# A fused deformable-convolution, attention and expert block: joined edits in the group norm, the hats, the tap products and the gated experts

## The chip, the core and the metric

The kernel runs on one core of one Trainium2 chip. Its engines are TensorE (PE; its weight loads are listed apart as PEld), VectorE (DVE), ScalarE (ACT), GpSimd (POOL) and SyncE (SP), which here only issues DMAs. Each engine works through its own list of instructions, and semaphores tie the lists together. The metric is device microseconds of one execution, the median of several runs. The kernel before takes 83.26 us.

## What is computed

The input x is 8 images of 16x16 pixels with 32 channels, all float32. Cut to what matters:

```python
x = x + conv(_gn(x), ...)          # group norm: each channel of each image over its 256 pixels
t = to_tokens(x)
t = t + attention(_ln_t(t))        # scores x x^T, softmax, weighted sum, per image
t = t + experts(_ln_t(t), ...)     # 8 experts of 32x32, the best two of each token, gated

def conv(x, ...):                  # a deformable 3x3 convolution, 8 groups of 4 channels
    x_proj = x @ w_in + b_in
    x1 = gelu(layer_norm(depthwise_3x3(x) + dw_b) * ln_g + ln_b)
    offset = x1 @ w_off + b_off                    # 8 groups x 9 taps x 2 coordinates
    mask = softmax((x1 @ w_msk + b_msk), over the 9 taps)
    # each tap reads x_proj at its place plus its offset, bilinearly; weighted by mask, summed
    return out @ w_out + b_out
```

## The kernel before

All data stay on the chip. The program is written out by hand: five lists, one for each engine, in the order in which they run, with a semaphore for each hand-over. Nothing schedules them afterwards, so an instruction that waits holds up all that stand behind it on its engine. The stages that the change touches are these.

**Group norm** (5 to 11 us of the trace). TensorE transposes the rows. VectorE takes BN_STATS of even and odd segments into `x_stats`. TensorE's `over_segments` (L552) averages the segment means by a product with `chan_mean` (x_mean). VectorE forms `x_dev`, its square `x_devsq` (L1095) and `x_segvar` (L1096, the segment variances plus these squares); TensorE averages that (x_var), ScalarE makes `gn_rstd` from it, and VectorE scales all columns to `xnT` in one instruction (L1102). Then TensorE runs the depthwise convolution as 12 products (L576). Between its real products stand warm products, whose results nobody reads (`keep_warm`, L538, counts in `WARM`). A float32 product is two records in the trace.

**Hats** (20 to 28 us). Bilinear weights of an offset o are the hats max(o,0), max(-o,0) and 1-|o|. The 16 image columns come in four chunks. VectorE makes the mask logits and the upper hat of each chunk; ScalarE makes the exponentials, |o| (`magnitudes`) and, for chunks 2 and 3 (`ACT_LOWER`), the lower hat (L923); POOL makes the middle hats and the lower hats of chunks 0 and 1. VectorE's first weight product (L309, `first_my`) waits for all of them; POOL and ScalarE then feed VectorE's second one.

**Taps** (28 to 51 us). For each of five tap rows `ty`, VectorE forms weights (`weights(i)`, L313), TensorE adds them up and turns them (`add_weights(ty)`, L643), VectorE multiplies them with the images (`products(ty)`, L1144, in pieces given by `PIECES[ty]`) and TensorE adds the products up (`add_row(ty)`, L654). Row 3 (`PAIRED`) is added in pairs on POOL (L510). `products(ty)` waits for `coef_done` of its row; each piece releases TensorE. Afterwards TensorE goes on to the tokens (L694, L718).

**Gated experts** (72 to 79 us). TensorE computes all experts of group n (L828). VectorE multiplies by the gates (`gated_experts`, L1346) for six n and ScalarE for n = 3 and 7 (L1026). VectorE sums four n over the experts (`sum_experts`, L1367) and POOL the other four in two lots (L529, L530). VectorE stores its gated values as [expert, channel]; ScalarE stores them as [channel, expert], where the eight addends lie side by side. The last result is L1382; its DMA follows.

## Time and profile before

| | us |
|---|---|
| median of 3 runs | 83.26 (83.23 to 83.63) |
| the profiled execution, its own time | 83.83 |
| its span, first to last instruction | 82.1 |
| TensorE busy | 70.6 (86%) |
| VectorE busy | 54.7 (67%) |
| POOL busy | 48.4 (59%) |
| ScalarE busy | 42.8 (52%) |

The span is what the rows below count in; 1.73 us of the profiled execution's time lie around it. TensorE's busy share holds all warm products, so it isn't the share of the work. The granted TensorE clock is full until 76 us and half from there on (0.964 on average).

### The profile page before, as it was taken

How to read it: one execution, taken by the hardware profiler on the slowest of the kernel's cores; microseconds unless marked ns; L12 is line 12 of the kernel's file. 1: busy time of each engine (PE TensorE's matmuls, PEld its weight loads, DVE VectorE, ACT ScalarE, POOL GpSimd, SP SyncE). 2: the span in 40 equal slices, each digit the busy share in tenths (PEclk: the TensorE clock that was granted, in tenths of full speed). 3: DMA queues.
4: the chain of work that ended last, by engine and by line, in shares of the span. 5: the costliest groups of instructions: out<-in, count | busy, mean ns of one | idle time of the engine just before them, and what ended most of it. 6: DMA issues, size and time to landing. Idle time of an engine off the chain costs nothing.

```text
span 82.1 us, 1760 instructions
## 1 busy us (share of the span) xinstructions
PE 70.6 (86%) x655; PEld 58.5 (71%) x655; DVE 54.7 (67%) x103; ACT 42.8 (52%) x141; POOL 48.4 (59%) x78
## 2 busy tenths in 40 slices
PE   1999999999599999899799999997797989999600
PEld 1989879867399988698799989775444767666200
DVE  1141530363996899999997996646235758999950
ACT  0353200499669256969994000365993430299910
POOL 5107089998599699999999997000003500248920
PEclk9999999999999999999999999999999999999555
DMA  0412182004870000000000000000000000000014
GB/s 0 131 43 57 26 168 28 10 8 140 241 198 0 8 4 0 0 0 4 0 0 8 4 0 0 0 0 8 0 0 0 0 0 8 0 0 0 0 33 95
DMA packets 5607, 2.51 MB, mean 31 GB/s; under 512 B 4623, under 2 KB 5135, under 8 KB 5599
## 3 DMA queue, kind: packets, MB, share of 16 engines
q1 hardware_dynamic: 4895, 2.14, 10.8%
q10 hardware_dynamic: 704, 0.26, 1.2%
q8 instruction: 5, 0.08, 0.4%
q14 instruction: 3, 0.02, 0.1%
HBM read 0.95 MB, written 0.26 MB: 15 GB/s over the span
## 4 chain that ended last, share of the span: by engine, by line
PE 26%; DVE 25%; ACT 5%; issue 3%; POOL 2%; POOLq 1%; DVEq 0%
PE ps L654 10%; DVE prod L313 6%; DVE image_all L1144 6%; DVE image_all L1346 4%; PE ps L643 4%; PE ps L775 3%; ACT image_all L1002 3%; POOL image_all L529 2%; PE ps L785 2%; PE ps L793 2%; PE ps L756 1%; DVE prod L1367 1%; PE ps L694 1%; PE ps L718 1%; PE ps L702 1%
## 5 line engine op out<-in xcount | busy, mean ns | idle before, releaser
L538 PE MATMUL ps<-wide_ident 128*128 128x128 f32 x104 | 15.8, 309 | 1.8 <-POOL wide_ident L396 1.8
L538 PEld LDWEIGHTS ps<-wide_ident 128*128 128x128 f32 x104 | 14.3, 218 | 3.2 <-POOL wide_ident L396 1.8
L1144 DVE TENSOR_TENSOR image_all<-ps,images 128x896 f32<-128x896 f32 (+4 forms) x8 | 13.2, 1690 | 0.4 <-PE ps L643 0.4
L654 PE MATMUL ps<-wide_ident,image_all 128*128 128x128 f32 (+2 forms) x92 | 11.2, 275 | 0.9 <-DVE image_all L1144 0.9
L654 PEld LDWEIGHTS ps<-wide_ident,image_all 128*128 128x128 f32 (+2 forms) x92 | 10.0, 139 | 1.6 <-DVE image_all L1144 1.6
L643 PE MATMUL ps<-wide_ident,prod 128*128 128x128 f32 x81 | 9.9, 275 | 0.1
L520 POOL TENSOR_TENSOR prod<-prod,tok 128x256 f32<-128x256 f32 x2 | 1.9, 962 | 12.9 <-DVE prod L1296 12.9
L643 PEld LDWEIGHTS ps<-wide_ident,prod 128*128 128x128 f32 x81 | 8.8, 141 | 0.8 <-DVE prod L313 0.6
L309 POOL TENSOR_TENSOR my<-prob,hat 128x384 f32<-128x384 f32 x8 | 7.9, 1012 | 0.7 <-DVE ps L309 0.7
L313 POOL TENSOR_TENSOR prod<-my,hat 128x1152 f32<-128x1152 f32 x3 | 8.0, 2652 | 0.2
L313 DVE TENSOR_TENSOR prod<-ps,hat 128x1152 f32<-128x1152 f32 x6 | 7.9, 1350 | 0.1
L1026 ACT ACTIVATE image_all<-ps,gate_s 128x32 f32<-128x32 f32 x32 | 5.9, 358 | 1.5 <-DVE gate_s L1338 1.5
L828 PE MATMUL ps<-expert,prod 32*128 32x256 f32 x32 | 4.9, 397 | 0.1
L529 POOL TENSOR_TENSOR image_all<-image_all 128x512 f32<-128x512 f32 (+1 forms) x4 | 4.0, 997 | 1.4 <-DVE image_all L1346 1.1
L975 ACT ACTIVATE sampT<-ps 128x128 f32<-128x128 f32 x2 | 0.8, 398 | 7.8 <-PE ps L718 7.8
L943 ACT ACTIVATE ps<-my 128x384 f32<-128x384 f32 x5 | 2.5, 495 | 4.0 <-POOL my L309 3.2
L828 PEld LDWEIGHTS ps<-expert,prod 32*128 32x128 f32 x32 | 3.4, 184 | 0.8 <-DVE image_all L1346 0.4
L1346 DVE TENSOR_TENSOR image_all<-ps,gate_s 128x512 f32<-128x512 f32 x6 | 3.8, 682 | 0.0
L576 PE MATMUL ps<-conv_w,xnT 128*128 128x160 f32 (+1 forms) x24 | 3.8, 316 | 0.0
L576 PEld LDWEIGHTS ps<-conv_w,xnT 128*128 128x128 f32 x24 | 3.6, 190 | 0.2 <-issue 0.2
L1107 DVE TENSOR_REDUCE c_sum<-c_sq 128x8 f32<-128x256 f32 x2 | 0.7, 414 | 4.4 <-ACT c_sq L901 4.4
L970 ACT ACTIVATE x_ctok<-x_tok,x_mean_tok 128x32 f32<-128x32 f32 x16 | 3.5, 308 | 0.0
(199 smaller groups left out, 143.9 us busy)
## 6 DMA issues: line engine op xcount, KB each, us to landing
images<-images SPq DMA_DIRECT2D x2, 300.0 KB, 4.2
images<-images SPq DMA_DIRECT2D x2, 280.0 KB, 3.6
x_tok<-in_x SPq DMA_DIRECT2D x4, 64.0 KB, 3.6
x_rows<-in_x SPq DMA_DIRECT2D x1, 128.0 KB, 2.8
x_rows<-in_x ACTq DMA_DIRECT2D x1, 128.0 KB, 3.2
expert<-in_expert_w SPq DMA_DIRECT2D x4, 32.0 KB
out_dram<-prod SPq DMA_DIRECT2D x2, 64.0 KB, 2.2
out_dram<-prod ACTq DMA_DIRECT2D x2, 64.0 KB, 2.5
```

The source lines that it names most:

```text
L309: return engine.tensor_tensor(dst, prob[:, ky:NP:K, :], hat[:, NP + ky:2 * NP:K, dy, :], ALU.mult)
L313: return engine.tensor_tensor(prod[:, ky, dy].rearrange("p (k d) j -> p k d j", d=D), bcast(rows, 2, D), hat[:, ky:NP:K, :, :], ALU.mult)
L529: then(g.tensor_tensor(x[:, :, 0:n], x[:, :, 0:n], x[:, :, n:2 * n], ALU.add))
L538: pe.matmul(pbank(bank, P), ident, ident, start=True, stop=True)
L576: ins = pe.matmul(pbank(2, (hi - lo) * C, x0 * C), xnT[:, b, dy:dy + H, :], conv_w[:, dy, lo:hi, :], start=False, stop=(b == 3 and dy == K ...
L643: ins = pe.matmul(coef_rows(ty, tx, tx + 1), prod[:, ky, dy, kx * D + dx, :], ident, start=first[tx // 4], stop=((ky, dy) == PAIRS_OF_ROW[ ...
L654: ins = pe.matmul(ps[0:last, SAMPLED, c * NJ:(c + 1) * NJ], taps[:, ty % SLOTS, tx, c, 0:last], ident, start=(ty == 0 and tx == 0 and c == ...
L828: ins = pe.matmul(pbank(EXPERT[n], NE * C, h * NE * C), ln2T[q * C:(q + 1) * C, ga, h, :], expert4[q * C:(q + 1) * C, :, :], start=True, s ...
L970: ins = act.activation(x_ctok[:, t, :], x_tok[:, ga, n, h, :], ACT.Identity, bias=x_mean_tok[:, t:t + 1])
L1026: ins = act.activation(gated_by_channel(ga, q, q + 1)[:, h, :, e], pbank(EXPERT[n], C, (h * NE + e) * C), ACT.Copy, scale=gate_s[:, ga * G ...
L1144: v.tensor_tensor(taps[:, ty % SLOTS, t0:t1, :, y0 * NI:y1 * NI], bcast(coef_rows(ty, t0, t1).rearrange("p (t j) -> p t j", j=P)[:, :, y0 ...
L1346: v.tensor_tensor(gated[:, ga, q, :, :, :], pbank(EXPERT[n]).rearrange("p (h e c) -> p h e c", h=HALVES, e=NE), bcast(by_image[:, q, :, :] ...
```

## The change

1. **Group norm.** A second matrix `chan_mean_32` (`chan_mean` / 32) is made early on. TensorE averages the segments' own sums of squares with it right behind x_mean, into bank 5, and adds the average of `x_devsq` to the same sum later; `x_segvar` is gone. The warm products behind x_mean fall from 4 to 3 and the one ahead of the convolution goes. `xnT` is written in two halves, and the convolution's first two column blocks wait for the first half only.
2. **Hats.** The lower hat of chunk 2 goes from ScalarE to VectorE, behind its last upper hat, with a semaphore `vector_lower_ready` on which VectorE and POOL wait.
3. **Taps.** Row 0 is in three pieces (before two), rows 1 and 2 in two (before one). TensorE adds the first piece of row 2 ahead of `add_weights(4)`.
4. **Side work.** POOL's tile mask, its expert bias and five index rows (L452 to L466) move from ahead of the hats to behind the pair sums. VectorE's `w_mean` and `w_out_c` (L1188, L1189) go to ScalarE, behind `x_ctok`, as nine small instructions.
5. **Gated experts.** ScalarE makes a copy of the expert weights turned to [channel, expert]; n = 2 and 6 (`BY_CHANNEL`) use it, so that their gated values lie like ScalarE's. `gated_experts(5)` goes ahead of `sum_experts(2)`.

```diff
-PIECES = (((0, 2), (2, 5)), ((0, 5),), ((0, 5),), ((0, 5),), ((0, 2), (2, 4), (4, 5)))
+PIECES = (((0, 2), (2, 4), (4, 5)), ((0, 2), (2, 5)), ((0, 2), (2, 5)), ((0, 5),), ((0, 2), (2, 4), (4, 5)))
...
-        ACT_LOWER = (2, 3)
+        ACT_LOWER = (3,)
+        VECTOR_LOWER = 2
...
+        BY_CHANNEL = (2, 6)
...
-            over_segments(0, x_stats[:, :, 1], x_stats[:, :, 4]).then_inc(x_mean, 1)
+            over_segments(chan_mean, 0, x_stats[:, :, 1], x_stats[:, :, 4]).then_inc(x_mean, 1)
+            over_segments(chan_mean_32, GROUP_VAR, x_stats[:, :, 2], x_stats[:, :, 5], last=False)
             keep_warm(7, WARM["squares"])
             pe.wait_ge(x_segments, 1)
-            over_segments(64, x_segvar[:, :, 0], x_segvar[:, :, 1]).then_inc(x_var, 1)
+            over_segments(chan_mean, GROUP_VAR, x_devsq[:, :, 0], x_devsq[:, :, 1], first=False).then_inc(x_var, 1)
...
-            keep_warm(7, WARM["normalised"])
             pe.wait_ge(conv_w_ready, 1)
             pe.wait_ge(consts, 3)
-            pe.wait_ge(x_normed, 1)
             for b in range(4):
+                pe.wait_ge(x_normed, 1 + b // 2)
...
             add_weights(3)
+            pe.wait_ge(taps_ready, pieces_ready(2, 0))
+            add_taps(2, range(*PIECES[2][0]))
             add_weights(4)
-            add_row(2)
+            add_row(2, done=1)
...
                 magnitudes(ch)
-                if ch in ACT_LOWER[:-1]:
-                    lower_hats(ch)
...
-            then(v.tensor_tensor(x_devsq[:, :, :], x_dev[:, :, :], x_dev[:, :, :], ALU.mult))
-            v.scalar_tensor_tensor(out=x_segvar[:, :, :], in0=x_stats[:, :, 2:6:3], scalar=1.0 / 32, in1=x_devsq[:, :, :],
-                                   op0=ALU.mult, op1=ALU.add).then_inc(x_segments, 1)
+            v.tensor_tensor(x_devsq[:, :, :], x_dev[:, :, :], x_dev[:, :, :], ALU.mult).then_inc(x_segments, 1)
+            v.wait_ge(x_segments, 1)
...
-            v.tensor_tensor(xnT[:, :, 1:1 + H, :], xc,
-                            gn_rstd[:, :].unsqueeze(1).unsqueeze(1).to_broadcast([P, 4, H, NI]), ALU.mult).then_inc(x_normed, 1)
+            for half in range(2):
+                b = slice(2 * half, 2 * half + 2)
+                v.tensor_tensor(xnT[:, b, 1:1 + H, :], xc[:, b],
+                                gn_rstd[:, :].unsqueeze(1).unsqueeze(1).to_broadcast([P, 2, H, NI]), ALU.mult).then_inc(x_normed, 1)
...
+            v.wait_ge(abs_ready, VECTOR_LOWER + 1)
+            v.tensor_scalar(hats_of(VECTOR_LOWER, 0), offsets_of(VECTOR_LOWER), -1.0, 0.0, ALU.mult, ALU.max).then_inc(vector_lower_ready, 1)
+            v.wait_ge(vector_lower_ready, 1)
...
-            v.wait_ge(late_ready, 2)
-            then(v.tensor_reduce(w_mean[:, :], w_out_bd[:, :, :], AX, ALU.add))
-            v.scalar_tensor_tensor(out=w_out_c[:, :, :], in0=bcast(w_mean[:, :], 2, C), scalar=-1.0 / C, in1=w_out_bd[:, :, :],
-                                   op0=ALU.mult, op1=ALU.add).then_inc(w_out_c_ready, 1)
...
             gated_experts(4)
+            gated_experts(5)
             sum_experts(2)
-            gated_experts(5)
             sum_experts(3)
```

The order of the instructions shows three of these places. The first is TensorE in the group norm, from the second block of warm products to the convolution. L538 is a warm product, L555 and L556 are `over_segments`, L566 is the convolution's bias and L576 the convolution. Before:

```order
L538 MATMUL ps<-wide_ident 128x128 x5
L555 MATMUL ps<-x_stats,chan_mean 128x8
L556 MATMUL ps<-x_stats,chan_mean 128x8
L538 MATMUL ps<-wide_ident 128x128 x4
L555 MATMUL ps<-x_segvar,chan_mean 128x8
L556 MATMUL ps<-x_segvar,chan_mean 128x8
L566 MATMUL ps<-centring,conv_bias 128x512
L538 MATMUL ps<-wide_ident 128x128
L576 MATMUL ps<-conv_w,xnT 128x160 x3
```

After, with the new line numbers (L544 warm, L561 and L562 `over_segments`, L573 bias, L582 convolution):

```order
L544 MATMUL ps<-wide_ident 128x128 x5
L561 MATMUL ps<-x_stats,chan_mean 128x8
L562 MATMUL ps<-x_stats,chan_mean 128x8
L561 MATMUL ps<-x_stats,chan_mean 128x8
L562 MATMUL ps<-x_stats,chan_mean 128x8
L544 MATMUL ps<-wide_ident 128x128 x3
L561 MATMUL ps<-x_devsq,chan_mean 128x8
L562 MATMUL ps<-x_devsq,chan_mean 128x8
L573 MATMUL ps<-centring,conv_bias 128x512
L582 MATMUL ps<-conv_w,xnT 128x160 x3
```

Two small products came in between x_mean and the variance's second part, one warm product left that place, and another left the place ahead of the convolution.

The second place is TensorE from the flag product (L678) to the end of the taps. L643 adds weights, L654 adds taps. Before:

```order
L678 MATMUL ps<-ones,over_all 1x1
L654 MATMUL ps<-wide_ident,image_all 128x128 x20
L643 MATMUL ps<-wide_ident,prod 128x128 x27
L654 MATMUL ps<-wide_ident,image_all 128x128 x20
L654 MATMUL ps<-wide_ident,image_all 120x128 x4
L654 MATMUL ps<-wide_ident,image_all 112x128 x20
L654 MATMUL ps<-wide_ident,image_all 120x128 x8
```

After (L686 the flag product, L649 weights, L660 taps):

```order
L686 MATMUL ps<-ones,over_all 1x1
L660 MATMUL ps<-wide_ident,image_all 128x128 x20
L649 MATMUL ps<-wide_ident,prod 128x128 x18
L660 MATMUL ps<-wide_ident,image_all 128x128 x8
L649 MATMUL ps<-wide_ident,prod 128x128 x9
L660 MATMUL ps<-wide_ident,image_all 128x128 x12
L660 MATMUL ps<-wide_ident,image_all 120x128 x4
L660 MATMUL ps<-wide_ident,image_all 112x128 x20
L660 MATMUL ps<-wide_ident,image_all 120x128 x8
```

Eight of row 2's twenty tap records now stand ahead of the last nine weight records; no record was added.

The third place is VectorE in the last stage. Before, L1346 is `gated_experts`, L1367 `sum_experts`, L1382 the last result:

```order
L1338 TENSOR_TENSOR gate_s<-second,top 128x128
L1346 TENSOR_TENSOR image_all<-ps,gate_s 128x512 x4
L1367 TENSOR_REDUCE prod<-image_all 128x64
L1346 TENSOR_TENSOR image_all<-ps,gate_s 128x512
L1367 TENSOR_REDUCE prod<-image_all 128x64
L1346 TENSOR_TENSOR image_all<-ps,gate_s 128x512
L1367 TENSOR_REDUCE prod<-image_all 128x64 x2
L1382 TENSOR_TENSOR prod<-ps,prod 128x2x4x32
```

After (L1369 `gated_experts` of a `BY_CHANNEL` group, L1372 of another, L1391 `sum_experts`, L1406 the last result):

```order
L1360 TENSOR_TENSOR gate_s<-second,top 128x128
L1372 TENSOR_TENSOR image_all<-ps,gate_s 128x512 x2
L1369 TENSOR_TENSOR image_all<-ps,gate_s 128x512
L1372 TENSOR_TENSOR image_all<-ps,gate_s 128x512 x2
L1391 TENSOR_REDUCE prod<-image_all 128x64 x2
L1369 TENSOR_TENSOR image_all<-ps,gate_s 128x512
L1391 TENSOR_REDUCE prod<-image_all 128x64 x2
L1406 TENSOR_TENSOR prod<-ps,prod 128x2x4x32
```

The fifth gated group moved ahead of the first sum; the counts are the same.

## Rows read from the trace of the kernel before

**Rows 1.** The page: the chain that ended last, by line

```profile
PE ps L654 10%; DVE prod L313 6%; DVE image_all L1144 6%; DVE image_all L1346 4%; PE ps L643 4%; PE ps L775 3%; ACT image_all L1002 3%; POOL image_all L529 2%; PE ps L785 2%; PE ps L793 2%; PE ps L756 1%; DVE prod L1367 1%; PE ps L694 1%; PE ps L718 1%; PE ps L702 1%
```

**Rows 2.** Timeline of VectorE, group norm: start us, duration us, instruction [idle before <-releaser]

```profile
8.86 0.17 DVE L1096 SCALAR_TENSOR_TENSOR x_segvar<-x_stats,x_devsq 128x16 f32<-128x16 f32 x1
10.35 0.69 DVE L1102 TENSOR_TENSOR xnT<-x_cent,gn_rstd 128x512 f32<-128x512 f32 x1 [0.71 <-ACT gn_rstd L879]
```

**Rows 3.** Timeline of TensorE's weight loads, 5 to 11.3 us

```profile
5.32 2.21 PEld L538 LDWEIGHTS ps<-wide_ident 128*128 128x128 f32 x10
...
8.08 0.97 PEld L538 LDWEIGHTS ps<-wide_ident 128*128 128x128 f32 x8
9.09 0.30 PEld L555 LDWEIGHTS ps<-x_segvar,chan_mean 128*128 128x128 f32 x2
...
10.68 0.30 PEld L538 LDWEIGHTS ps<-wide_ident 128*128 128x128 f32 x2 [0.76 <-issue]
11.16 0.30 PEld L576 LDWEIGHTS ps<-conv_w,xnT 128*128 128x128 f32 x2 [0.18 <-issue]
```

**Rows 4.** Timelines of POOL and VectorE where both work in SBUF

```profile
10.49 1.10 POOL L425 TENSOR_SCALAR proj_b<-proj_b_raw 128x144 f32<-128x144 f32 x1 [2.50 <-DMA proj_b_raw<-in_b_msk]
...
11.98 0.69 POOL L425 TENSOR_SCALAR proj_w<-proj_raw 128x144 f32<-128x144 f32 x1
...
49.90 0.84 POOL L514 TENSOR_SCALAR tok<-x_tok 128x256 f32<-128x256 f32 x1
...
50.12 0.32 DVE L1189 SCALAR_TENSOR_TENSOR w_out_c<-w_mean,w_out_bd 128x128 f32<-128x128 f32 x1
```

**Rows 5.** Timelines of VectorE and ScalarE, end of the hats

```profile
25.28 0.74 DVE L1135 TENSOR_SCALAR hat<-ps 128x576 f32<-128x576 f32 x1
...
26.06 0.65 ACT L923 ACTIVATE hat<-ps 128x576 f32<-128x576 f32 x1
...
26.91 0.57 DVE L309 TENSOR_TENSOR ps<-prob,hat 128x384 f32<-128x384 f32 x1 [0.88 <-ACT hat L923]
...
29.26 1.36 DVE L313 TENSOR_TENSOR prod<-ps,hat 128x1152 f32<-128x1152 f32 x1
```

**Rows 6.** Timeline of VectorE, the tap products

```profile
31.80 1.08 DVE L1144 TENSOR_TENSOR image_all<-ps,images 128x896 f32<-128x896 f32 x1
...
32.80 1.55 DVE L1144 TENSOR_TENSOR image_all<-ps,images 128x1344 f32<-128x1344 f32 x1
...
43.90 2.66 DVE L1144 TENSOR_TENSOR image_all<-ps,images 128x2400 f32<-128x2400 f32 x1 [0.41 <-PE ps L643]
```

**Rows 7.** Timeline of TensorE's weight loads in the taps

```profile
39.49 2.17 PEld L654 LDWEIGHTS ps<-wide_ident,image_all 128*128 128x128 f32 x20 [0.58 <-DVE image_all L1144]
...
43.78 0.96 PEld L643 LDWEIGHTS ps<-wide_ident,prod 128*128 128x128 f32 x9 [0.15 <-issue]
...
47.61 0.84 PEld L654 LDWEIGHTS ps<-wide_ident,image_all 128*112 128x112 f32 x8 [0.25 <-DVE image_all L1144]
48.61 2.15 PEld L654 LDWEIGHTS ps<-wide_ident,image_all 128*112 128x112 f32 x20 [0.16 <-DVE image_all L1144]
```

**Rows 8.** Timelines of VectorE, ScalarE and POOL in the last stage

```profile
74.28 1.03 DVE L1367 TENSOR_REDUCE prod<-image_all 128x64 f32<-128x512 f32 x1
...
75.84 0.67 DVE L1367 TENSOR_REDUCE prod<-image_all 128x64 f32<-128x512 f32 x1
...
78.80 0.42 DVE L1382 TENSOR_TENSOR prod<-ps,prod 128x256 f32<-128x256 f32 x1
...
73.52 4.30 ACT L1026 ACTIVATE image_all<-ps,gate_s 128x32 f32<-128x32 f32 x24
...
76.00 2.08 POOL L529 TENSOR_TENSOR image_all<-image_all 128x512 f32<-128x512 f32 x2
78.15 0.45 POOL L530 TENSOR_TENSOR prod<-image_all 128x128 f32<-128x128 f32 x1
```

**Rows 9.** Timeline of TensorE behind its longest pause in the first half

```profile
22.29 0.63 PE L669 MATMUL ps<-wide_ident,images 128*128 128x128 f32 x4 [1.01 <-ACT absoff L919]
```

97 lines of the change are left out of this document (59 added, 38 removed).

## The prediction
> **What bounds the kernel now.** I read the chain of waits first. Its largest parts are TensorE's tap sums, VectorE's weight and tap products and the gated experts [rows 1]; no engine carries it alone, so an edit is worth what it takes from the wait that ends last at its own place. I then read each of the four places in the timelines, TensorE by its weight loads, because a load shows when TensorE could really go on, while its matmuls' ends are modelled.
>
> Group norm: the loads of the variance start at 9.09, 0.06 us after `x_segvar` ended (8.86 + 0.17), so VectorE sets them [rows 2, 3]. The convolution's first load is at 11.16, 0.12 after the end of `xnT` (10.35 + 0.69 = 11.04) [rows 2, 3]. Hats: VectorE idles 0.88 us, from 26.02 to 26.91, until ScalarE's last lower hat ends (26.06 + 0.65 = 26.71) [rows 5]. Taps: TensorE stands still for VectorE ahead of row 1 (0.58), row 4's first piece (0.25) and its second (0.16), and 0.15 ahead of the last weights [rows 7]; VectorE stands still for TensorE once, 0.41 ahead of `products(3)` [rows 6]. So the end of the taps hangs on the pieces of row 4, these on `products(3)`, and that on TensorE, which had lost its time waiting for row 1. Last stage: VectorE runs without a gap up to the last result at 78.80; POOL's last sum ends at 78.60, ScalarE's last gated group at 77.82 [rows 8].
>
> **Group norm: -0.23 us.** TensorE's loads of small or warm products follow each other every 0.11 us: eight take 0.97 with 0.19 for the last one alone, (0.97 - 0.19) / 7 [rows 3]. Between 8.08 and the variance stood 8 loads; now there are 4 + 6 = 10, which end at 8.08 + 10 x 0.11 = 9.20. `x_devsq`, which ends before 8.86, no longer sets the place. So the variance starts 0.11 us later, not 0.17 earlier, although VectorE's instruction is gone, and `xnT` starts at 10.46. An instruction of VectorE costs a fixed 0.15 plus 1.04 ns for each element: (1.55 - 1.08) / 448 = 1.04 ns, and 1.08 - 896 x 1.04 ns = 0.15 [rows 6]. Half of `xnT` (256 elements) is thus 0.42, ends at 10.88, and the first load can come at 10.93. TensorE would be free then: the load behind the bias was at 10.68 [rows 3] and comes 0.11 later, 10.79. The gain is 11.16 - 10.93 = 0.23. It ends at 0.06 if the 0.12 between `xnT` and the load becomes 0.29 by the new waits, and at 0.34 if the added loads fit in ahead of 9.09; 0.23 goes by the load spacing, which repeats in each row. The second half ends 0.4 us later than the first, while the first two blocks keep TensorE busy for longer than that (12 loads, over 1.3 us). What follows (squares, layer norm, Gelu, projections, logits) is one chain from the end of the convolution and moves as a whole.
>
> **Hats: +0.05 us.** ScalarE loses the lower hat of chunk 2, but its last lower hat starts at 26.06, right when VectorE's last upper hat ends (25.28 + 0.74 = 26.02), for which it waits [rows 5]. So it doesn't move, and this part takes away nothing. VectorE pays 0.74 for the hat that it takes over (same shape and source as its upper hats), inside the idle 0.88 [rows 5]; it would end at about 26.7, with ScalarE's 26.71. What is left is the added wait. From ScalarE's 26.71 to 26.91 lie 0.20 us in which VectorE works off its other waits [rows 5], at most 0.1 for one; POOL, which feeds VectorE's second weights at 29.26 by way of ScalarE, has one more as well. Bounds 0 and 0.1, I take 0.05. Without the cover the hat would cost its whole 0.74.
>
> **Taps: -0.25 us.** A further piece costs VectorE 0.06: two instructions in a row start 32.80 - 31.80 = 1.00 apart, of which 896 x 1.04 ns = 0.93 are elements [rows 6]. Three more pieces ahead of `products(3)` make 0.18. VectorE was free at 43.90 - 0.41 = 43.49 and now is at 43.67. TensorE gains 0.5 at row 1, which can start at about 39.0 in place of 39.49 [rows 7]; the first eight of its records last until the second piece is there. It would release `products(3)` at about 43.4. VectorE is later, so `products(3)` starts at 43.67 rather than 43.90, -0.23, and with it row 4's pieces and TensorE's last 20 records, which wait for the second one [rows 7]. I take 0.25, since 0.02 of the three-piece cost stood ahead of a wait. Row 2's first eight records, moved ahead of the last weights, fill the 0.15 in which TensorE waited there [rows 7]; they aren't on the path now, and neither is the earlier release. Bounds: 0 if a piece costs its fixed 0.15 (three make 0.45, more than the 0.41), and 0.5 if VectorE's pieces overlap fully.
>
> **Side work: 0.** POOL's moved block ends about 2 us later than its work there did; its next customer needs `tok` at 62 us. ScalarE's new instructions stand where it idles for several us before the sampled rows. VectorE's two instructions end at 50.44 [rows 4], before TensorE's last taps are through: 48.61 + 2.15 = 50.76 [rows 7]. If that cover is gone, they'd be worth 0.5 more.
>
> **Last stage: -0.24 us.** A sum whose addends lie 32 apart takes 1.03, one with neighbours 0.67 [rows 8]: two sums save 0.36 each, 0.72 of VectorE's time. But the last sum needs ScalarE's last gated group, at 73.52 + 4.30 = 77.82 [rows 8], which nothing in the change moves. It starts at 77.87, ends at 78.54, and the last result starts at 78.57 rather than 78.80. POOL's second lot started at 76.00 and ended at 78.60 [rows 8]; with group 5 earlier it starts when the first lot ends, 0.18 us earlier, and ends at 78.42. So 0.23 to 0.24 of the 0.72 count. Bounds: 0.1 if POOL stays at 78.60 and 0.25 at best.
>
> **Sum.** -0.23 + 0.05 - 0.25 - 0.24 = -0.67 us. The profiled execution took 83.83, of which 82.1 are the span; its span would be 81.4 and its time 83.16. It lies 0.57 above the median of the runs, and I take the difference from the median: 83.26 - 0.67 = **82.59 us**.
>
> **Rivals.**
>
> Rival A, POOL ahead of `xnT`. POOL's L425 reads SBUF at 10.49, VectorE's `xnT` (two SBUF operands) started 0.14 before it; POOL's instruction then took 1.10, its twin without a neighbour 0.69 [rows 4]. Now the margin shrinks to 10.49 - 10.46 = 0.03. If POOL is first and VectorE has to wait for its end (10.49 + 0.69 = 11.18), the first half ends at 11.60 and the convolution loads at 11.65: +0.49 in place of -0.23, and the time is 82.59 + 0.72 = 83.31. Against it: L1189, with two SBUF operands too, started at 50.12 in the middle of POOL's L514 (49.90 to 50.74) and took 0.32, where 0.15 + 128 x 1.04 ns = 0.28 were due [rows 4, 6]. It hardly waited. 11%.
> The Trainium skill (SBUF — State Buffer, "SBUF: two separate sides") has it that VectorE with two SBUF inputs and a GpSimd instruction share a port pair as an exclusive lock, held for the whole instruction by whichever started first. By that rule rival A's 83.31 holds; the trace agrees for POOL behind VectorE (1.10 for 0.69) and not for VectorE behind POOL (0.32).
>
> Rival B, the pieces eat the taps' gain. If a piece costs 0.15, VectorE reaches `products(3)` at 43.94, no earlier than before: 82.59 + 0.25 = 82.84. For it: the duration has that fixed part. Against it: starts 1.00 apart. 13%.
>
> Rival C, the taps follow TensorE. If the pieces cost VectorE nothing, `products(3)` starts at 43.4: 82.59 - 0.25 = 82.34. 10%.
>
> Rival D, slower: the clock is lost ahead of the convolution. One warm product fewer stands there, and one fewer ahead of the variance. At TensorE's slower rate ten loads took 2.21, (2.21 - 0.2) / 9 = 0.22 each, at the faster 0.11 [rows 3]. The convolution's 24 records would take twice their 3.75 us: 82.59 + 3.75 = 86.3. It decides if a pause of 0.1 to 0.2 us between bias and convolution is enough. Against it: loads already paused there from about 10.9 to 11.16, and after a pause of 1.01 us four records still took 0.63 [rows 9]. 6%.
>
> **How the numbers follow.** The forecast gets 60%, its own range is 82.3 to 82.95: taps and group norm can each fail or exceed by 0.15 to 0.2. Runs of this kernel differ by about 0.5%, 0.42 us, so faster means under 82.84. Of the forecast's 0.60, 0.55 lie below and 0.05 above; C gives 0.10; B's 0.13 splits into 0.03 and 0.10; A's 0.11 is within 0.5%; D's 0.06 is slower. Faster 0.68, same 0.26, slower 0.06. The range goes from 82.2, which takes in C, to 83.1, which takes in B with a weaker last stage; A and D, 0.17, lie outside.
>
> **What would show it.** Group norm: the variance's loads at about 9.2, `xnT` in two rows of 0.42 from 10.46 and the first convolution load at 10.93; a first half of over 0.5 or a start behind POOL's L425 is rival A. Hats: no idle of VectorE over 0.25 before its first weights, which start 26.9 less the 0.23. Taps, counted without the earlier shift: `products(3)` at 43.67 with next to no idle before it; idle before it would mean that TensorE still sets it, as in C. The row 4 loads still wait for VectorE. Last stage: all sums 0.67, the last one idle for about 0.4 before it, released by ScalarE. I'm wrong in kind if the order of these stages' gains differs, above all if the hats give or take more than 0.1 us.

## The result, and the profile after

| | median | executions | lowest, highest |
|---|---|---|---|
| before | 83.25 us | 6 | 83.05, 83.63 |
| changed | 83.21 us | 6 | 81.86, 84.62 |

The six times of the changed kernel are 81.86, 81.96, 82.00 and 84.42, 84.61, 84.62: two groups with nothing between. The comparison takes the short ones alone: ratio 0.9853 with an interval of 0.9809 to 0.9897, which puts the changed kernel at about 82.0 us, below my range of 82.2 to 83.1. The runs below show that the long ones come from the change, and their traces speak against the short ones being a fair half of the kernel's executions.

The profiled execution is a long one, 84.62 us with a span of 82.9. Its page differs from the page before in one line that matters, the granted TensorE clock in 40 slices, before and after:

```profile
PEclk9999999999999999999999999999999999999555
```

```profile
PEclk9999965999999999999999999999999999999955
```

In stretches (us of the stretch, then busy time of PE, PEld, DVE, ACT and POOL with instruction counts, granted clock, DMA share and GB/s):

```profile
10.00:10.50 0.50, 0.50 (x2) 0.00 (x0) 0.29 (x1) 0.10 (x1) 0.00 (x0) 1.00 0.21 40
10.50:11.00 0.50, 0.33 (x2) 0.26 (x2) 0.46 (x2) 0.00 (x0) 0.21 (x1) 0.80 0.51 111
11.00:12.00 1.00, 1.00 (x5) 1.00 (x6) 0.00 (x0) 0.00 (x0) 1.00 (x3) 0.50 1.12 230
12.00:14.00 2.00, 2.00 (x8) 2.00 (x8) 0.00 (x0) 0.00 (x0) 1.94 (x5) 0.50 0.35 54
14.00:15.00 1.00, 1.00 (x7) 1.00 (x7) 0.00 (x0) 0.00 (x0) 0.94 (x2) 0.89 0.14 14
```

The clock is at half (1.2 GHz) from just before the convolution until past 14 us, then full again (2.4 GHz). This is rival D's mechanism, with an end that I had not given it. TensorE's matmuls at that place, and the same 24 in an execution of this kernel without the fall (the one of 82.73 us below):

```profile
10.78 5.49 PE L582 MATMUL ps<-conv_w,xnT 128*128 128x160 f32 x24 [0.17 <-DVE xnT L1125]
```

```profile
10.55 3.82 PE L582 MATMUL ps<-conv_w,xnT 128*128 128x160 f32 x24 [0.17 <-DVE xnT L1125]
```

The kernel was measured again twice. Of 19 executions in all, 7 took 84.4 to 84.8 us with a mean granted clock of 0.956 to 0.958, 4 took 82.26 to 82.73 with 0.961 to 0.964, and 8 took 81.9 to 82.2 with 0.977 to 0.981. The kernel before, in 71 executions beside these and the other runs, never took over 83.9: 27 between 83.2 and 83.9 at 0.960 to 0.969, 44 between 82.6 and 83.6 at 0.970 and above. I call an execution long and count a fall in it by its time and this mean; the fall itself is seen in the two long executions of this kernel that were profiled. The third measurement was profiled in an execution of 82.73 us, span 81.0, clock at half only at the end:

```profile
PEclk9999999999999999999999999999999999999555
```

**One table for all traces.** The chain passes through the same operations of VectorE in every kernel, so I took the distances between their starts: `x_dev` (the mean is there) to `xnT`, to the first `c_sum` (the convolution is through), to the first `y_weights` product, to the reciprocal behind the taps, to `samp`, to `gate_s`, to the last addition. "Ahead" is the start of `x_dev` itself. All in us.

| kernel | ahead | to xnT | to c_sum | to y_weights | to reciprocal | to samp | to gate_s | to last | behind x_dev |
|---|---|---|---|---|---|---|---|---|---|
| before | 8.37 | 1.98 | 5.11 | 11.45 | 22.09 | 2.04 | 20.52 | 7.24 | 70.43 |
| changed, 84.62 | 8.11 | 2.10 | 6.51 | 11.49 | 21.79 | 2.03 | 20.51 | 7.04 | 71.47 |
| changed, 82.73 | 7.88 | 2.10 | 4.84 | 11.49 | 21.79 | 2.02 | 20.52 | 7.04 | 69.80 |

Where the kernel and its clock are the same, the distances repeat from trace to trace within 0.02 us, while whole executions of one kernel differ by over 1 us. With the clock full, the changed kernel gains 70.43 - 69.80 = 0.63 us behind `x_dev`. In the long execution the same work loses 1.04, because 1.67 are added in the convolution (6.51 for 4.84).

The places of the prediction, in the trace of 82.73 us. Weight loads that answer to [rows 3]:

```profile
8.04 0.75 PEld L544 LDWEIGHTS ps<-wide_ident 128*128 128x128 f32 x6
8.71 0.30 PEld L561 LDWEIGHTS ps<-x_devsq,chan_mean 128*128 128x128 f32 x2
...
9.26 0.29 PEld L573 LDWEIGHTS ps<-centring,conv_bias 32*128 32x128 f32 x2
10.52 3.60 PEld L582 LDWEIGHTS ps<-conv_w,xnT 128*128 128x128 f32 x24 [0.97 <-issue]
```

VectorE at the hats and ScalarE's last lower hat, [rows 5] before, here from the trace of 84.62 us, 1.30 us later as a whole:

```profile
26.55 0.75 DVE L1158 TENSOR_SCALAR hat<-ps 128x576 f32<-128x576 f32 x1
27.21 0.75 DVE L1182 TENSOR_SCALAR hat<-ps 128x576 f32<-128x576 f32 x1
28.21 0.57 DVE L313 TENSOR_TENSOR ps<-prob,hat 128x384 f32<-128x384 f32 x1 [0.25 <-ACT hat L934]
```

```profile
27.33 0.65 ACT L934 ACTIVATE hat<-ps 128x576 f32<-128x576 f32 x1 [0.22 <-DVE hat L1158]
```

The tap products there, [rows 6]: no idle time ahead of the four products from 44.91 on, where 0.41 us stood.

```profile
42.05 2.88 DVE L1167 TENSOR_TENSOR image_all<-ps,images 128x1024 f32<-128x1024 f32 x2
44.85 0.14 DVE L1206 TENSOR_SCALAR flag<-ps 1x1 int32<-1x1 f32 x1
44.91 5.16 DVE L1167 TENSOR_TENSOR image_all<-ps,images 128x2400 f32<-128x2400 f32 x4
```

The last stage in the trace of 82.73 us, [rows 8]: the sums take 0.67 (two in 1.27) and 0.69 us, and the last one waits 0.29 us for ScalarE.

```profile
74.08 1.27 DVE L1391 TENSOR_REDUCE prod<-image_all 128x64 f32<-128x512 f32 x2
75.27 0.68 DVE L1369 TENSOR_TENSOR image_all<-ps,gate_s 128x512 f32<-128x512 f32 x1
75.98 0.69 DVE L1391 TENSOR_REDUCE prod<-image_all 128x64 f32<-128x512 f32 x1
76.95 0.69 DVE L1391 TENSOR_REDUCE prod<-image_all 128x64 f32<-128x512 f32 x1 [0.29 <-ACT image_all L1047]
77.68 0.42 DVE L1406 TENSOR_TENSOR prod<-ps,prod 128x256 f32<-128x256 f32 x1
```

### The profile page after: what moved, and what is told of

It is laid out like the page before. It is cut to its first block, busy times and chain, and to the rows that moved or that the text cites. A ratio compares the mean times of both kernels' runs of the same rounds, so it can differ in the third digit from the quotient of the medians.

```text
span 82.9 us, 1777 instructions
## 1 busy us (share of the span) xinstructions
PE 71.1 (86%) x655; PEld 59.7 (72%) x655; DVE 54.6 (66%) x106; ACT 44.9 (54%) x154; POOL 48.1 (58%) x78
## 3 DMA queue, kind: packets, MB, share of 16 engines
q1 hardware_dynamic: 4895, 2.14, 10.8%
## 4 chain that ended last, share of the span: by engine, by line
DVE 27%; PE 16%; ACT 12%; issue 5%; DVEq 0%
DVE image_all L1167 11%; DVE prod L317 8%; ACT image_all L1047 7%; PE ps L660 4%; PE ps L785 3%; ACT image_all L1023 3%; PE ps L795 2%; PE ps L803 2%; PE ps L766 1%; PE ps L704 1%; PE ps L728 1%; DVE prod L1391 1%; PE ps L712 1%; PE ps L721 1%; PE ps L756 1%
## 5 line engine op out<-in xcount | busy, mean ns | idle before, releaser
L544 PE MATMUL ps<-wide_ident 128*128 128x128 f32 x100 | 15.0, 308 | 1.8 <-POOL wide_ident L400 1.8
L544 PEld LDWEIGHTS ps<-wide_ident 128*128 128x128 f32 x100 | 13.8, 219 | 2.4 <-POOL wide_ident L400 1.8
L1167 DVE TENSOR_TENSOR image_all<-ps,images 128x896 f32<-128x896 f32 (+6 forms) x11 | 13.3, 1263 | 0.0
L660 PE MATMUL ps<-wide_ident,image_all 128*128 128x128 f32 (+2 forms) x92 | 11.2, 275 | 0.3 <-DVE image_all L1167 0.3
L660 PEld LDWEIGHTS ps<-wide_ident,image_all 128*128 128x128 f32 (+2 forms) x92 | 10.0, 139 | 0.9 <-DVE image_all L1167 0.7
L649 PE MATMUL ps<-wide_ident,prod 128*128 128x128 f32 x81 | 10.0, 274 | 0.5 <-DVE prod L317 0.4
L649 PEld LDWEIGHTS ps<-wide_ident,prod 128*128 128x128 f32 x81 | 8.9, 141 | 1.2 <-DVE prod L317 0.6
L582 PEld LDWEIGHTS ps<-conv_w,xnT 128*128 128x128 f32 x24 | 5.3, 264 | 1.0 <-issue 1.0
L582 PE MATMUL ps<-conv_w,xnT 128*128 128x160 f32 (+1 forms) x24 | 5.5, 406 | 0.2 <-DVE xnT L1125 0.2
L460 POOL TENSOR_SCALAR hat<-absoff 128x576 f32<-128x576 f32 x3 | 2.0, 682 | 4.2 <-ACT absoff L930 4.2
L838 PE MATMUL ps<-expert,prod 32*128 32x256 f32 x24 | 4.3, 396 | 0.1
L912 ACT ACTIVATE c_sq<-ps 128x256 f32<-128x256 f32 x2 | 0.7, 382 | 6.2 <-PE ps L582 6.2
L970 ACT ACTIVATE tok_q<-x_tok 128x32 f32<-128x32 f32 x16 | 3.4, 214 | 0.0
```

Source lines behind the costliest of these rows:

```text
L544: pe.matmul(pbank(bank, P), ident, ident, start=True, stop=True)
L582: ins = pe.matmul(pbank(2, (hi - lo) * C, x0 * C), xnT[:, b, dy:dy + H, :], conv_w[:, dy, lo:hi, :], start=False, stop=(b == 3 and dy == K ...
L649: ins = pe.matmul(coef_rows(ty, tx, tx + 1), prod[:, ky, dy, kx * D + dx, :], ident, start=first[tx // 4], stop=((ky, dy) == PAIRS_OF_ROW[ ...
L660: ins = pe.matmul(ps[0:last, SAMPLED, c * NJ:(c + 1) * NJ], taps[:, ty % SLOTS, tx, c, 0:last], ident, start=(ty == 0 and tx == 0 and c == ...
L838: ins = pe.matmul(pbank(EXPERT[n], NE * C, h * NE * C), ln2T[q * C:(q + 1) * C, ga, h, :], (expert_by_channel if n in BY_CHANNEL else expe ...
L970: ins = act.activation(tok_q[:, t, :], x_tok[:, ga, n, h, :], ACT.Copy, accum_out=x_mean_tok[:, t:t + 1])
```

## The experiments

### Is it the group norm that makes the clock fall?

Theory 1: the group norm's edits, and in them the two warm products that they drop.

**The changed kernel again.** No edit.

> The changed kernel once more, unaltered, as the measure for the three beside it. Theory 1 (the group norm's edits let TensorE's clock fall to half ahead of the convolution in some executions and not in others): two kinds of executions again, near 81.9 to 82.0 us and near 84.4 to 84.6 us, nothing between; where the profiled one is of the short kind, its granted clock is 1.00 from 10 to 20 us, the convolution's 24 products take 3.8 us as before and not 5.5. Rival (what splits the times has nothing to do with the clock around 11 us): the convolution's products take the same in both kinds, and the difference of 2.5 us lies elsewhere.

Measured: 81.92, 82.07, 82.18, 82.63 and 84.58, 84.58, 84.83 us. The profiled one is a long one again, 8.62 us from `x_dev` to `c_sum` as in the first trace (8.61). The value of 82.63 is the first of a middle group, which I had not expected.

**The changed kernel with the old group norm.**

```diff
-            over_segments(chan_mean_32, GROUP_VAR, x_stats[:, :, 2], x_stats[:, :, 5], last=False)
-            over_segments(chan_mean, GROUP_VAR, x_devsq[:, :, 0], x_devsq[:, :, 1], first=False).then_inc(x_var, 1)
+            over_segments(64, x_segvar[:, :, 0], x_segvar[:, :, 1]).then_inc(x_var, 1)
...
+            keep_warm(7, WARM["normalised"])
```

(and one warm product more ahead of the variance, VectorE's segment variances, `xnT` in one.)

> The changed kernel with the group norm of the kernel before (VectorE adds the segment variances, one operation for the normalised input, four and one warm products). Theory 1: one kind of executions only, no fall of the clock at 10.8 us; time = the short kind of the changed kernel plus the group norm's gain. That gain is 0.23 us by my sum and 0.42 us by the trace of the changed kernel (first weight load of the convolution at 10.74 against 11.16), so 82.2 to 82.4 us. Rival (the clock falls for something else in the change): both kinds stay, 82.3 and 84.8.

Measured: twelve executions, 82.25 to 83.37 us, median 83.10 where I had expected 82.2 to 82.4, none long; ratio to before 0.9966 (0.9929 to 1.0003). The long ones are gone with the group norm. The spread of 1.1 us was no part of my expectation; it is the kernel before's own (82.6 to 83.9). By distances the trace gives 1.98, 5.11, 11.49, 21.79, 2.02, 20.51, 7.03: the group norm is exactly the old one and the other stages exactly the changed ones, 69.93 behind `x_dev` against 70.43.

**The changed kernel with the old warm products.**

```diff
-WARM = {"start": 5, "group sums": 5, "squares": 3, "hats": 30, "layer norm": 2,
+WARM = {"start": 5, "group sums": 5, "squares": 4, "hats": 30, "layer norm": 2,
...
                       skip_group_check=True)
+            keep_warm(7, 1)
             pe.wait_ge(conv_w_ready, 1)
```

> The changed kernel with the warm products of the kernel before: four behind the means of the group norm in place of three, and one behind the bias product ahead of the convolution. Theory 1: the long executions are gone, all within 81.9 to 82.1 us, since TensorE idles behind the warm products anyway and they delay nothing by more than 0.1. Rival (it is the four more small loads or the earlier convolution, and not the fewer warm products, that makes the clock fall): both kinds stay.

Measured: thirteen executions, ten from 82.04 to 82.98 us and three at 84.98 to 84.99. Theory 1 falls in this form: the dropped warm products are not what it takes. They also weren't free: `x_dev` to `xnT` is 2.32 here against 2.10, since the fourth product stands ahead of the variance.

**The group norm's edits alone**, on the kernel before.

> The kernel before with the group norm's edits alone (variances summed in a bank by TensorE, two halves of the normalised input, three warm products and none). Theory 1: two kinds; the short one at the kernel before's 83.25 minus 0.2 to 0.4, so 82.85 to 83.05, and the long one 2.5 us above. Rival (the edits of the group norm move the start but the middle waits for something else, hats or offsets): the short kind at 83.25.

Measured: twelve executions, ten from 82.55 to 83.20 and two at 84.83 and 85.03; ratio of the others 0.9970 (0.9940 to 0.9999). So the edits of the group norm are enough to make the clock fall. Its distances to `c_sum`, 2.10 and 4.84, are those of the changed kernel: 6.94 against 7.09, a gain of 0.15.

### What in the group norm does it?

What is left of the edits is the one more pair of small products (four records of a 128x128 weight load each, for 8 columns). Theory 2: they take the place of 128x128 products ahead of the convolution, and with them there the clock falls.

**The kernel before with one more such pair**, read by nobody.

```diff
             over_segments(0, x_stats[:, :, 1], x_stats[:, :, 4]).then_inc(x_mean, 1)
+            small = chan_mean[:, :, :].rearrange("p q c -> p (q c)")
+            pe.matmul(pbank(5, NI), small, x_stats[:, :, 2], start=True, stop=False)
+            pe.matmul(pbank(5, NI), small, x_stats[:, :, 5], start=False, stop=True)
             keep_warm(7, WARM["squares"])
```

> The kernel before with one more pair of small products (four loads and four products of 8 columns, into a bank that nobody reads) behind the means, ahead of its four warm products. Nothing else differs. Theory 2: a part of the executions shows the clock at half from about 11 us and takes about 85.5 us, which no run of the kernel before does; the others are 0.2 to 0.4 us above the kernel before, since the warm products behind the small ones end later than VectorE's segment variances. Rival (small products do not matter to the clock): one kind of executions, 83.4 to 83.6.

Measured: eleven executions from 82.93 to 83.72 us, two at 85.56 and 85.71. All the warm products of the kernel before are there, `xnT` is in one piece, and the clock falls all the same in two of thirteen, where none of the 71 executions without that pair was long. Its weight loads ahead of the convolution, and the clock in the stretches behind:

```profile
7.37 0.54 PEld L555 LDWEIGHTS ps<-x_stats,chan_mean 128*128 128x128 f32 x2
7.79 0.34 PEld L556 LDWEIGHTS ps<-x_stats,chan_mean 128*128 128x128 f32 x2
8.05 0.30 PEld L562 LDWEIGHTS ps<-x_stats,chan_mean 128*128 128x128 f32 x2
8.28 0.30 PEld L563 LDWEIGHTS ps<-x_stats,chan_mean 128*128 128x128 f32 x2
8.50 0.97 PEld L538 LDWEIGHTS ps<-wide_ident 128*128 128x128 f32 x8
```

```profile
9.50:11.00 1.50, 1.50 (x9) 0.72 (x7) 0.45 (x2) 0.48 (x2) 0.00 (x0) 1.00 0.21 42
11.00:12.00 1.00, 1.00 (x5) 0.82 (x5) 0.35 (x1) 0.00 (x0) 0.41 (x1) 0.64 1.13 234
```

**The changed kernel with its pauses filled**: the bias product in place of the warm products ahead of the variance, five warm products behind it.

```diff
-            keep_warm(7, WARM["squares"])
-            pe.wait_ge(x_segments, 1)
-            over_segments(chan_mean, GROUP_VAR, x_devsq[:, :, 0], x_devsq[:, :, 1], first=False).then_inc(x_var, 1)
             pe.wait_ge(vec_cols_ready, 2)
             pe.wait_ge(centring_ready, 1)
             pe.matmul(pbank(2), conv_bias[:, :], bcast(centring[0:C, :], 1, W), start=True, stop=False,
                       skip_group_check=True)
+            pe.wait_ge(x_segments, 1)
+            over_segments(chan_mean, GROUP_VAR, x_devsq[:, :, 0], x_devsq[:, :, 1], first=False).then_inc(x_var, 1)
+            keep_warm(7, 5)
```

> The changed kernel with the four more small loads kept, but TensorE's pauses filled: the bias product in place of the three warm products ahead of the variances, five warm products behind the variances up to the convolution. Theory 2 (what counts is how much product work there is between the clock's rise and the convolution): no execution above 83.4 us, also those whose clock rises late (mean clock 0.964 to 0.968); the variances 0.2 us later than in the changed kernel, so 82.1 to 83.1 us. Rival (the small loads as such do it): a third to a half of the executions at 84.6 us or more.

Measured: five of six executions at 84.14 to 84.88 us, one at 82.53. My expectation is turned round: TensorE's matmuls follow each other without a pause up to the convolution (the loads pause only while the bias product runs, 0.76 us, as in the kernel before), and the clock falls more often and earlier. In its trace `x_dev` is at 7.42, and the clock falls behind a row of small products, the bias product (32 of 128 rows) and small products again. Weight loads:

```profile
7.36 0.30 PEld L562 LDWEIGHTS ps<-x_stats,chan_mean 128*128 128x128 f32 x2
7.68 0.29 PEld L570 LDWEIGHTS ps<-centring,conv_bias 32*128 32x128 f32 x2
8.73 0.30 PEld L561 LDWEIGHTS ps<-x_devsq,chan_mean 128*128 128x128 f32 x2 [0.76 <-DVE x_devsq L1117]
8.95 0.30 PEld L562 LDWEIGHTS ps<-x_devsq,chan_mean 128*128 128x128 f32 x2
9.17 2.07 PEld L544 LDWEIGHTS ps<-wide_ident 128*128 128x128 f32 x10
```

The granted clock there, by stretches (it stands third from the end):

```profile
8.00:9.50 1.50, 1.50 (x8) 0.77 (x7) 0.69 (x1) 0.12 (x1) 0.00 (x0) 0.96 0.10 22
9.50:11.00 1.50, 1.50 (x9) 1.50 (x9) 0.76 (x2) 0.36 (x2) 0.00 (x0) 0.50 0.17 33
```

PE counts as busy for the whole 1.50 us of both stretches, with ends that are modelled, and the clock still goes from full to half between them. So neither a pause between matmuls nor the page's busy time tells of it. What TensorE did ahead of each fall, in all the traces with one, were the small products and the bias product, with the 128x128 products fewer or later than in the kernel before. It is not the later convolution as such: its first load stands at 10.74 us in the long execution of the changed kernel and at 11.16 in the kernel before, where the clock stays. That much the runs show; what the chip makes of the small products is open, and a pair of 128x128 products in their place, which would tell their few columns from the time they take, was not run.

**One pair in place of two.** Means and segment variances in one pair of products with 16 columns, the squares scaled by 32, four and one warm products:

```diff
+        group_sums = ps[:, 0, 0:2 * NI].rearrange("p (n s) -> p n s", s=2)
-            over_segments(chan_mean, 0, x_stats[:, :, 1], x_stats[:, :, 4]).then_inc(x_mean, 1)
-            over_segments(chan_mean_32, GROUP_VAR, x_stats[:, :, 2], x_stats[:, :, 5], last=False)
+            over_segments(chan_mean, group_sums, x_stats[:, :, 1:3], x_stats[:, :, 4:6], last=False).then_inc(x_mean, 1)
```

> The changed kernel with the segments' means and variances in one pair of products (16 columns for 8 and 8, the squares scaled by 32 on VectorE, the scale taken out in the root's logarithm), so without the four more small weight loads, and with four warm products and one as in the kernel before. Theory 2 (the clock falls because the four small loads take 0.44 us of the stretch between the clock's rise at 7.4 to 7.9 us and the convolution with almost no columns, and the convolution then starts later than that stretch): no execution above 83.5 us. The group norm from the mean's subtraction to the convolution's first sums takes 7.09 - 0.27 = 6.8 us, 0.15 less than the changed group norm's 6.94, so the short executions lie 0.1 below the changed kernel's, 81.8 us and up. Rival (it is the earlier half of the normalised input, hence the shorter stretch of warm work, that lets the clock fall): some executions near 84.5 us.

Measured: six executions, 81.69 to 82.61 us, none long; ratio 0.9891 (0.9838 to 0.9945). `x_dev` to `c_sum` is 6.72, the shortest of all kernels.

**The same with three warm products ahead of the variance.**

> The kernel of the run before this one with three warm products ahead of the variances instead of four. Theory 2: the squares are ready 0.46 us behind the mean, so the variance's load moves 0.2 us earlier than with four, and the short executions lie 0.1 to 0.2 us lower; with less work in the stretch some executions at 84.3 may come back, fewer than the changed kernel's 6 of 13. If warm products weighed as nothing, the share of long executions would be that of the run before this one.

Measured: six executions, 81.73 to 82.46 us, none long; ratio 0.9877 (0.9827 to 0.9928). `x_dev` to `xnT` is 2.08 and not shorter than with four (1.86), for a reason of its own that the next section gives.

**The changed kernel with one warm product behind the bias product.**

> The changed kernel with the one warm product behind the bias product put back, the three ahead of the variances left at three. Theory 2: it fills the idle 0.17 us and takes 0.24, so the convolution starts up to 0.1 us later, and the long executions become no more than with both restored (3 of 13), since the four small loads stay. Rival (the pause between bias product and convolution alone makes the clock fall): no long execution.

Measured: six executions, 81.93 to 82.54 us, none long. By itself that would speak for its rival, but it settles nothing. With one warm product more still, 3 of 13 were long, so none of six can be chance, and in its trace `x_dev` is at 7.52, earlier than in any trace of the changed kernel with a fall (8.07 to 8.34). The same reserve holds for the two runs before it (7.73 and 7.07). Its distances behind `x_dev` are those of the changed kernel (69.79 and 69.80), and with none of its executions long the ratio is 0.9894 (0.9844 to 0.9943), 82.4 us when taken of 83.25.

### VectorE and GpSimd at the same port

**Two operations of GpSimd let off with `xnT`**, for rival A, in the changed kernel.

```diff
+            g.wait_ge(gn_rstd_ready, 1)
+            for i in range(2):
+                g.tensor_tensor(spare[:, i, :], ident, ident, ALU.mult)
             g.wait_ge(consts, 3)
```

> The changed kernel with two extra operations of GpSimd (128x128, two operands in SBUF, results that nobody reads) let off by the same event as VectorE's normalised input. Theory 5 (VectorE's operation with two operands in SBUF stands still while GpSimd has one running; my rival A put this mechanism at GpSimd's projection weights, which start behind the normalised input): VectorE's first half is stretched from 0.42 us to 0.6 to 1.3 us, and the convolution starts 0.3 to 0.9 us later than in the changed kernel by its group norm (2.6 us from the mean's subtraction there). Rival (the two do not disturb each other, the long x_devsq had another cause): both halves stay at 0.42 us, and the convolution at 2.6 us.

Measured: the two halves of `xnT` take 1.19 us together, 0.76 without the neighbour, and the convolution's first load is at 10.77, 2.87 behind `x_dev` (2.64 in the trace of 82.73 us). The first half takes 0.66 in place of 0.43, so the delay of 0.23 is its own, somewhat less than the 0.3 to 0.9 that I had expected.

```profile
10.00 1.19 DVE L1129 TENSOR_TENSOR xnT<-x_cent,gn_rstd 128x256 f32<-128x256 f32 x2 [0.92 <-ACT gn_rstd L894]
```

```profile
9.98 0.94 POOL L429 TENSOR_TENSOR spare<-wide_ident 128x128 f32<-128x128 f32 x2 [2.04 <-ACT gn_rstd L894]
```

The mechanism of rival A is real. It just didn't strike where I had put it: in the changed kernel GpSimd's projection weights start at 10.79 in the first trace, behind the first half of `xnT`. In the second trace they start at 10.44, while the second half is due, and the two halves take 0.99 us together; that cost nothing, since `c_sum` came 8.62 behind `x_dev` as against 8.61. It strikes elsewhere, when the program starts early. From the group norm's edits alone, VectorE and GpSimd:

```profile
7.52 0.45 DVE L1098 TENSOR_TENSOR x_devsq<-x_dev 128x16 f32<-128x16 f32 x1
```

```profile
7.48 0.46 POOL L421 TENSOR_TENSOR w_in_bd<-w_in,quad_mask 128x128 f32<-128x128 f32 x1
```

`x_devsq`, 16 elements wide, takes 0.17 us in the traces in which it doesn't meet that operation. Here it started 0.04 behind GpSimd's operation and ended 0.03 behind it. In the kernel with row 1 in two pieces (below), which has the old group norm and an early start, `x_segvar` is hit, 0.32 for 0.17, and `x_dev` to `xnT` takes 2.12 and not 1.98.

The Trainium skill (SBUF — State Buffer, "SBUF: two separate sides") says that whoever of the two starts first holds the port pair for its whole instruction. The rows of `x_devsq` agree: VectorE ends with GpSimd's operation. My row against it, 0.32 in the middle of a long GpSimd operation [rows 4], is no exception of one trace. In the kernel with row 1 in two pieces the same operation ran in 0.29 us, wholly inside GpSimd's work on `tok`, and in that with the group norm's edits alone again in 0.29:

```profile
47.99 1.67 POOL L514 TENSOR_SCALAR tok<-x_tok 128x256 f32<-128x256 f32 x2
```

```profile
48.58 0.29 DVE L1189 SCALAR_TENSOR_TENSOR w_out_c<-w_mean,w_out_bd 128x128 f32<-128x128 f32 x1
```

So the rule does not hold for every such pair, and what sets these two apart stays unexplained.

### The middle and the last stage

**Row 1 in two pieces, alone**, in the kernel before.

```diff
-PIECES = (((0, 2), (2, 5)), ((0, 5),), ((0, 5),), ((0, 5),), ((0, 2), (2, 4), (4, 5)))
+PIECES = (((0, 2), (2, 5)), ((0, 2), (2, 5)), ((0, 5),), ((0, 5),), ((0, 2), (2, 4), (4, 5)))
```

> The kernel before with one edit: the tap products of row 1 in two pieces (columns 0 to 2, then 2 to 5), nothing else. Theory 3 (of the three rows cut in pieces only row 1 matters: TensorE waits 0.48 us for its products, and VectorE behind it 0.41 us for the weights of row 3): from VectorE's first y_weights product to its reciprocal of the denominators 22.09 - 0.41 + 0.07 = 21.75 us, against 22.09 before and 21.79 with all the cuts, and the wait of 0.41 us ahead of the product of row 3 is gone. Rival (the early piece of row 2 or the third piece of row 0 is needed too): 0.2 us or more of the wait stays, 21.95 us or above.

Measured, in one execution of 82.41 us: 21.66 us from `y_weights` to the reciprocal. The wait of 0.41 is gone:

```profile
42.32 0.14 DVE L1180 TENSOR_SCALAR flag<-ps 1x1 int32<-1x1 f32 x1
42.38 2.63 DVE L1144 TENSOR_TENSOR image_all<-ps,images 128x2400 f32<-128x2400 f32 x1
```

One cut does it. It even leads the full set of cuts at the reciprocal (21.66 against 21.79), and gives that back at `samp`, 2.14 against 2.02, since TensorE's taps end later without the early piece of row 2: 23.80 and 23.81 in sum, against 24.13 before.

**The last stage without the channel order.** Two runs, of which the first was made wrongly: it multiplies in the old order but reads without a stride, so it sums other elements than the reference does, and only its distances count (its one execution, 84.86 us, is one in which the clock fell).

```diff
-        BY_CHANNEL = (2, 6)
+        BY_CHANNEL = ()
```

> The changed kernel with no group multiplied in channel order (the two sums read with a stride again, the order of VectorE's operations kept as changed). Theory 4: the strided sum of 1.03 us comes back twice for 0.67, no wait for ScalarE ahead of the last sum stays (0.29 us in the changed kernel), and from gate_s to the last addition it takes 7.24 us as in the kernel before, against 7.03 changed. Rival (the order of the operations was worth something by itself): 7.1 us or less.

Measured: 7.04 us from `gate_s` to the last addition, as changed, with the wait of 0.29. For what it was meant to show it is a miss. What it shows is that the order in which the product is written costs nothing; only the sum's reading does. The second run also gives the sums their stride back:

```diff
+                strided = gated[:, ga, q, :, :, :].rearrange("p h e c -> p h c e")
-                v.tensor_reduce(moe[:, ga, q, :, :], gated_by_channel(ga, q, q + 1), AX, ALU.add).then_inc(vector_summed, 1)
+                v.tensor_reduce(moe[:, ga, q, :, :], gated_by_channel(ga, q, q + 1) if n in ACT_GATED else strided, AX, ALU.add).then_inc(vector_summed, 1)
```

> The changed kernel with the two groups gated and summed as in the kernel before, with a stride (this is what e10_strided_sums was meant to be), VectorE's order of operations as changed. Theory 4: sums of 1.03 and 0.67 where the changed kernel has 0.67 each, no wait of 0.29 us for ScalarE ahead of the last sum, 7.24 us from gate_s to the last addition (before 7.24, changed 7.04). Rival (the new order alone gives the gain): 7.05 us.

Measured: 7.38 us, 0.14 above what I had expected. The wait for ScalarE is gone and each pair of sums takes 1.64 or 1.63:

```profile
74.01 1.64 DVE L1392 TENSOR_REDUCE prod<-image_all 128x64 f32<-128x512 f32 x2
75.57 0.67 DVE L1372 TENSOR_TENSOR image_all<-ps,gate_s 128x512 f32<-128x512 f32 x1
76.28 1.63 DVE L1392 TENSOR_REDUCE prod<-image_all 128x64 f32<-128x512 f32 x2
```

The stride is worth 7.38 - 7.04 = 0.34, and the new order of VectorE's operations without it costs 0.14 against the kernel before (7.24). Why it costs that is open; together they make the 0.20.

### A version that keeps the gains and not the fall

**All that the runs pointed to**: the pair of 16 columns, the bias product ahead of the variance and five warm products behind, `w_in_bd` behind `x_devsq`, old lower hats, row 0 in two pieces.

> The changed kernel with what the runs so far point to: segment means and variances in one pair of products; the convolution's bias product ahead of the variances in place of warm products and five warm products behind them, so that TensorE has columns up to the convolution; GpSimd's w_in_bd let go behind VectorE's x_devsq; both lower hats on ScalarE as in the kernel before; row 0 in two pieces as before, rows 1 and 2 in two. Expected by segment: group norm from the mean's subtraction to the first conv sum 6.6 to 6.8 us (changed 6.94), c_norm to first y_weights 10.08 (changed 10.12), from there to the reciprocal 21.72 (changed 21.79), the rest as changed. No execution above 83 us; 81.4 to 82.3 us, median 81.8, against 81.9 to 84.8 of the changed kernel. Rival (the clock still falls in some executions, since it is not the work but the pause that counts): some at 84.

Measured: nine executions, 81.84 to 83.11 us, median 82.12, none long; ratio 0.9905 (0.9859 to 0.9951). The profiled execution has its `x_dev` at 8.34, as late as any trace with a fall (8.07 to 8.34 in the changed kernel), and keeps the clock:

```profile
9.50:11.00 1.50, 1.50 (x13) 1.34 (x13) 0.55 (x3) 0.48 (x2) 0.28 (x1) 1.00 0.30 61
11.00:12.00 1.00, 1.00 (x8) 0.99 (x8) 0.46 (x1) 0.00 (x0) 1.00 (x3) 1.00 1.14 231
```

With late executions among these nine, none with the fall speaks against the rival: the fall can be avoided. This kernel and the one with its pauses filled both have the bias product ahead of the variance and five warm products behind; the first has one pair of small products fewer and no long execution of nine, the second five of six (their other differences are not on TensorE there). But it isn't faster than the changed kernel's short executions: with the bias product ahead of the variance, `x_dev` to `xnT` takes 2.12, where four warm products had 1.86, so `x_dev` to `c_sum` is 6.97 and not the 6.6 to 6.8 that I had expected, and one execution lies above my 83. `y_weights` to the reciprocal is 21.72, as expected.

**The same, leaner**: three warm products ahead of the variance as changed, bias product behind, then two.

> The changed kernel with one pair of products for segment means and variances, three warm products ahead of the variances as changed and two behind the bias product, GpSimd's w_in_bd let go behind x_devsq, lower hats as before, row 0 in two pieces. Theory 2: enough work and fewer small loads; group norm from the mean's subtraction to the first conv sum 6.65 to 6.75 us (changed 6.94); no execution above 83 us; 81.5 to 82.7 us with the rise of the clock, 0.2 below e12_all_best at the same rise. Rival (three warm products and the bias product are too little when the clock rises late): a few executions at 84.2.

Measured: six executions, 81.78, 81.81, 81.81, 81.84, 82.09 and 82.82 us, none long; ratio 0.9844 (0.9803 to 0.9884), with all six executions in it. The changed kernel has 0.9853 to 0.9883 from its short executions alone, so the two can't be told apart there; what is gained is that no execution was long. With `w_in_bd` out of the way `x_devsq` takes 0.17 at an early start too, and `x_dev` to `xnT` is 1.77 where the run with three warm products had 2.08. The two warm products behind the bias hold the convolution up by 0.2 (5.08 for 4.86), and `x_dev` to `c_sum` is 6.85, above the 6.65 to 6.75 that I had expected. Median of all executions, with before at 83.42 beside it: 81.82 us. Whether its clock can fall is not sure after six executions; the trace is of an early one (`x_dev` at 7.11), the 82.82 may be of a later one.

**The changed kernel a third time**, beside it.

> The changed kernel once more, beside the three above. By the two earlier measurements: about half of the executions at 84.4 to 84.8 us with a mean clock of 0.956 to 0.958, the others at 81.9 to 82.2 (0.977 to 0.981) and 82.6 (0.964). If the theory of the early rise holds, the short ones are those in which x_dev comes at 7.1 to 7.9 us (8.1 in the profiled long ones), and a kernel before with the same rise would take 82.7 to 83.3, so 0.7 to 0.8 us more.

Measured: 81.90, 82.00, 82.26, 82.48, 82.73 and 84.56 us: one long one of six, where I had expected half. Its trace is the one of 82.73 us above.

## Why the prediction was right and wrong

**The sum was right: -0.67 forecast, -0.63 measured** behind `x_dev` with the clock full. It is that close in part by luck: the group norm gave 0.08 less than its term and the taps 0.07 more.

- Group norm, -0.23: measured -0.15. The variance does start later, and by the spacing of the loads: 0.83 behind `x_dev` (8.71 - 7.88) against 0.72, so 0.11 as worked out. The half of `xnT` saves its 0.26 (0.43 for 0.69). Most of what the term is off by is the step from `xnT` to the first load: I gave it 0.05, and it took 0.11 (9.98 + 0.43 = 10.41, load at 10.52) where the kernel before has 0.12.
- Hats, +0.05: measured +0.04, VectorE idle for 0.25 ahead of its first product, released by ScalarE.
- Taps, -0.25: measured -0.30 to the reciprocal, -0.32 to `samp`. `products(3)` follows `flag` at once, so VectorE sets it, not TensorE. A further piece cost 0.07. Rivals B and C are out. That row 1 was the wait that counted is shown by the run with that cut alone.
- Side work, 0: 20.51 us from `samp` to `gate_s`, 20.52 before.
- Last stage, -0.24: measured -0.20, bounded by ScalarE's last gated group as worked out.

**Two steps failed: rival D, and the step from the sum to the time.** Rival D I gave 6% and held against it that a pause of 1.01 us elsewhere had not slowed the products behind it [rows 9], and that loads already paused ahead of the convolution. Both looked at pauses. In the filled kernel no such pause was left and the clock fell; with one more pair of small products it fell in the kernel before too. These I had counted only as 0.11 us of delay for each load. The price was too high as well: I let all 24 records run at half clock, 3.75 us; in fact the clock came back within the convolution, and the long executions lose 1.67 there.

The time I got as "83.26 - 0.67", which takes it that every execution moves by the sum. The executions of one kernel spread over 1.2 us, and of the changed kernel's only a part went into the ratio: 82.0 measured for 82.59, with -0.63 of work for my -0.67. The median of all its 19 executions, long ones included, is 82.48, inside my range, but that is the luck of the mix and not the sum.

**Why 82.0 and not 82.6.** The start of the program differs from execution to execution. The ten warm loads behind the transposes take 2.21 us in the profiled execution of the kernel before [rows 3], 1.97 in the changed kernel's of 82.73, and 1.19 to 1.32 in the traces with `x_dev` at 7.1 to 7.2. The changed kernel's of 82.73 us, and that of the kernel before with row 1 in two pieces, which is the same up to the taps:

```profile
5.26 1.97 PEld L544 LDWEIGHTS ps<-wide_ident 128*128 128x128 f32 x10
```

```profile
5.18 1.19 PEld L538 LDWEIGHTS ps<-wide_ident 128*128 128x128 f32 x10
```

TensorE goes over to its faster rate earlier or later in that row, and `x_dev` moves with it, from 7.07 to 8.37 over all traces. The change of rate is read from the loads; the granted clock reads 1.00 from the start of the traces on and doesn't show it. So one kernel spreads over 1.2 us (before: 82.6 to 83.9).

In the changed kernel it is the executions with a late change of rate in which the clock then falls: `x_dev` at 8.07, 8.11 and 8.34 in its traces (the last with the sums altered) and at 8.23 with the old warm products. In the four traces of its group norm without a fall, `x_dev` is at 7.88, at 7.90 and 7.81 with edits elsewhere, and at 7.52 with one warm product more. So the late ones drop out of the lower group, and what stays in it are executions with an early start. The kernel with that one warm product more fits: the same work, none dropped, 82.4; its interval is too wide to prove it.

The ratio of 0.985 compares the short executions with all of the kernel before's. Lowest with lowest it is 82.63 and 81.86, -0.77; of that, 0.63 are the sum above, and 0.14 may be the port: with an early start the old group norm has `x_segvar` in GpSimd's way (2.12 for 1.98), the new one loses nothing by it, as its variance waits for loads (2.10). This last step is read from traces of three kernels and wasn't tested alone. Nor is the account closed: the medians of the groups with the higher mean clock, 82.97 (44 executions before) and 81.98 (8 of the changed kernel), lie 0.99 apart, and no run shows that the two hold the same starts.

The Trainium skill (TensorE: Matmul & The Clock Gate, "Part 1: The HAM clock gate") says that the chip's look at TensorE's activity runs free of the kernel's start, so that the place of the change differs from run to run. The spread of the ten loads agrees, 1.19 to 2.21 us.

## What to carry to other kernels

Compare stages by distances between the same operations in two traces, and look at the spread of whole executions before a change of half a per cent is read from a median. Where TensorE is kept warm by filler, small products that are put in its row are not only their own delay: look at the granted clock behind them in several executions, since one profile may show none of it. And where VectorE's and GpSimd's small operations in SBUF can meet, order them by a wait that costs nothing.

## What the runs showed that I had not expected

- The clock fell from full to half in stretches in which PE counts as busy without a break (1.50 of 1.50 us on both sides).
- Going by times and mean clocks, it fell in 7 of 19 executions of the changed kernel and in none of 71 of the kernel before, with four small loads more (0.45 us) and two warm products fewer between the two.
- VectorE's operation of 16 elements took 0.45 us beside one of GpSimd, 0.17 alone.
- The same instructions up to `x_dev` took 8.37 us in one execution and 7.13 in another (the kernel before, and that with row 1 in two pieces).
- A VectorE operation with two operands in SBUF ran undisturbed, 0.29 us, inside a GpSimd operation, while others waited for theirs to end.
